# The turns of Q and K behind the last product with V and behind the ones pass, in a gated cross-attention and expert kernel

## The reference

```python
x = x + tanh(g_xattn) * attention(ctx, layernorm(x), b, seq_len)
x = x + tanh(g_ffn) * experts(layernorm(x), w1, b1, w2, b2, centroids, w_route)

logits = einsum('bhqd,bhkd->bhqk', Q * dh**-0.5, K) + b        # masked by seq_len
out = einsum('bhqk,bhkd->bhqd', softmax(logits), V)
```

## Time and profile before

| what | value |
|---|---|
| median of three runs | 1841.51 us |
| the profiled execution's own time | 1838.65 us |
| its span, first to last instruction | 1836.9 us |
| mean granted TensorE clock | 0.987 of full speed |
| TensorE busy with matmuls | 94% of the span |
| VectorE, ScalarE, GpSimd busy | 74%, 65%, 67% |
| from one ones pass to the next, steps with g = 0, 1, 2, 3 | 19.33, 19.12, 18.60, 18.57 us |

### The profile page before, as it was taken

The page is one execution under the profiler, slowest core; times in us unless marked ns, Lnnn a source line. Parts: engine busy times, 40 slices in busy tenths (PEclk is TensorE's granted clock), DMA queues, the critical chain, the costliest instruction groups (busy, mean ns, idle before and its releaser), DMA issues. The chain is left out here.

```text
span 1836.9 us, 33094 instructions
## 1 busy us (share of the span) xinstructions
PE 1718.4 (94%) x9714; PEld 1038.6 (57%) x9715; DVE 1364.6 (74%) x3007; ACT 1190.2 (65%) x2049; POOL 1224.8 (67%) x1395
## 2 busy tenths in 40 slices
PE   1699999999999999999999999999499999999997
PEld 1344545555555555555555555553378887878876
DVE  4677878878778788887887887773666776767765
ACT  4267677676776767767677676767256666666664
POOL 1257667585675857758577576654368888888886
PEclk9999999999999999999999999999599999999999
DMA  5979899898998989889889897974468888887784
GB/s 118 173 129 188 155 181 170 144 197 162 172 178 136 209 151 172 186 128 210 151 170 187 128 207 106 186 128 145 128 134 170 154 160 160 177 155 150 153 164 75
DMA packets 173099, 291.45 MB, mean 159 GB/s; under 512 B 38014, under 2 KB 42110, under 8 KB 172976
## 3 DMA queue, kind: packets, MB, share of 16 engines
q1 hardware_dynamic: 138704, 219.88, 62.1%
q0 software_dynamic: 32960, 67.68, 18.5%
q10 hardware_dynamic: 1312, 2.38, 0.8%
HBM read 127.09 MB, written 71.63 MB: 108 GB/s over the span
## 5 line engine op out<-in xcount | busy, mean ns | idle before, releaser
L1157 DVE TENSOR_REDUCE bank<-bank 128x1 f32<-128x512 f32 x1024 | 696.0, 690 | 255.0 <-PE bank L906 246.9
L751 ACT ACTIVATE prob<-bank 128x512 f32<-128x512 f32 x1024 | 593.1, 597 | 355.2 <-PE bank L894 354.1
L655 POOL TENSOR_TENSOR prob<-prob 128x512 f32<-128x512 f32 x252 | 315.8, 1294 | 319.0 <-PE bank L828 319.0
L894 PE MATMUL bank<-stB,stack_a_then_w_hi 100*128 100x512 f32 x1024 | 476.0, 466 | 16.0 <-ACT prob L751 13.7
L906 PE MATMUL bank<-stack_a_then_w_hi,stB 98*128 98x512 f32 x1024 | 423.1, 415 | 35.0 <-DMA stack_a_then_w_hi<-regrouped_then_w 19.7
L894 PEld LDWEIGHTS bank<-stB,stack_a_then_w_hi 100*128 100x128 f32 x1024 | 193.2, 189 | 248.4 <-ACT prob L751 176.3
L659 POOL TENSOR_TENSOR prob<-prob 128x512 f32<-128x512 f32 x252 | 315.5, 1295 | 0.0
L828 PE MATMUL bank<-prob,vin 128*32 128x512 f32 x2048 | 272.7, 605 | 0.7 <-ACT prob L751 0.7
L1429 POOL DMA_INDIRECT out_dram<-yout,scatter_ids x144 | 227.8, 1582 | 50.2 <-issue 38.1
L906 PEld LDWEIGHTS bank<-stack_a_then_w_hi,stB 98*128 98x128 f32 x1024 | 197.8, 193 | 84.7 <-DVE bank L1157 40.0
L1402 POOL DMA_INDIRECT rows_in<-xn_rows,gather_ids x152 | 181.6, 1195 | 71.5 <-issue 43.7
(11 more groups left out here) (202 smaller groups left out, 2160.7 us busy)
## 6 DMA issues: line engine op xcount, KB each, us to landing
stB<-regrouped_then_w SPq DMA_DIRECT2D x192, 256.0 KB, 5.7
stack_a_then_w_hi<-regrouped_then_w SPq DMA_DIRECT2D x183, 256.0 KB, 6.5
x_k_then_w<-in_x_dram SPq DMA_DIRECT2D x16, 1024.0 KB, 7.9
x_k_then_w<-in_ctx_dram SPq DMA_DIRECT2D x16, 1024.0 KB, 11.0
vin<-in_ctx_dram SPq DMA_DIRECT2D x16, 1024.0 KB, 8.7
xres<-in_x_dram SPq DMA_DIRECT2D x16, 1024.0 KB, 6.4
out_dram<-xres SPq DMA_DIRECT2D x16, 1024.0 KB, 7.2
xn_rows<-xn SPq DMA_DIRECT2D x60, 256.0 KB, 5.4
```

The lines of the kernel that those rows point to most:

```text
L655: pool.tensor_tensor(first[:, j, :], first[:, j, :], more[:, j, :], ALU.add).then_inc(s_acc, 1)
L751: act.activation(prob_of(st, 0, u)[:, j, :], psS[j % 2][:, :], ACT.Exp).then_inc(s_exp, 1)
L894: pe.matmul(psS[j % 2][:, :], stA[0:100, g, j, kt * P:(kt + 1) * P], stB[0:100, g, j, :], start=True, stop=True).then_inc(s_qk, 1)
L1157: dve.tensor_reduce(mx[:, s // 4, s % 4:s % 4 + 1], psM[s % 2][:, :], AX.X, ALU.max).then_inc(s_mx, 1)
```

## The change

The turn of Q moves from slot 0 to slot 1, where it stands behind the product with V. The turn of K moves from slot 3 to slot 2, where it stands behind the ones pass. ScalarE's copy of the turned Q moves from slot 0 to slot 1 and VectorE's low part of Q from slot 1 to slot 2; both keep their places for K. Nothing is added or taken away.

```diff
@@ ScalarE
-                        if s in (0, 4) and st.on(3):
+                        if s in (1, 4) and st.on(3):
                             evac_turned(st, s // 4)
@@ TensorE
                             values(st, -1, NT - 1)
                         if s == 2 and st.on(-1):
                             sums(st, -1)
-                        if s in (0, 3) and st.on(3):
-                            turn_rows(st, s // 3)
+                        if s in (1, 2) and st.on(3):
+                            turn_rows(st, s - 1)
@@ VectorE
-                        if s in (1, 5) and st.on(3):
+                        if s in (2, 5) and st.on(3):
                             lo_part(st, s // 5)
```

## The result

The changed kernel takes 1876.04 us (median of four runs, 1874.39 to 1876.36), the kernel before on the same occasion 1841.15 us: a ratio of 1.0189, 95% interval 1.0176 to 1.0203. That is 34.9 us slower. The profiled execution has a span of 1874.6 us.

What follows compares the result with a forecast made beforehand. TensorE was taken as the engine to follow, held in runs of three pairs by ScalarE and VectorE. Terms 16.1 (TQ) + 19.2 (TK) + 1 (fill) = 36.3 us gave 1877.8 us, range 1860 to 1889 (own range 1869 to 1886).

Steps and rivals of the forecast that it cites:

- The run of three costs what the turn saves: Step's border and behind the ones pass: third pair waits for its readers, so leaving out TQ saves 0.08 us, TK 0.07.
- The step 61 of the kernel before: Step with all pairs but no TQ or TK, taken as model: 1.93 us slot 15 to V, 3.82 ones pass to V.
- The turn behind narrow tiles adds 0.39 us: Behind V and the ones pass: V to turn 0.99, turn to next product 0.41, 1.40 us together against 1.00.
- The kinds of step: TQ at the border: +0.31 us in ordinary steps, +0.06 into g = 2, +0.39 into g = 1; TK +0.32 everywhere.
- The first steps: Steps 1 to 60 priced by g alone, fifteen of each kind for TQ, 0.32 us each for TK.
- The fill: Steps -3 to 0: TK waits for VectorE, 1 to 1.5 us per step; priced 0 to 5 us together, 1 taken.
- TK finds its bank free: Behind the ones pass: VectorE's low part of Q frees TQ's bank 0.4 us before TK's turn, so no wait.
- The base: Profiled execution's 1838.65 us plus 36.3 gives 1874.95; the median of runs lies 2.86 us higher, giving 1877.8.
- The rival with one costly place: Only one of the two places hurts, so only TK's 19 us remain: 1861 us, chance 0.12.
- the bank's wait: Rival: TK waits 0.3 us for TQ's bank in each of 60 steps, +18 us, 1896 us; chance 0.09.
- the rival of a full TensorE: Order is only bookkeeping; each of 120 turns saves 0.45 us and costs 0.39: -7 us, 1834.3 us, chance 0.04.

Runs made afterwards that it cites:

- q_only: Against the kernel before, only the turn of Q moves behind the V product, with its copy and low part; K keeps slot 3: 1858.19 us against 1841.56.
- k_only: Against the kernel before, only the turn of K moves behind the ones pass; Q keeps slot 0: 1858.08 us against 1841.56.
- q_ahead_of_v: Against the kernel before, Q is turned in slot 1 ahead of the V product, its copy and low part as in q_only; K keeps slot 3: 1868.85 us, ratio 1.0156.
- after_short_both: Changed kernel with maxima and exponentials over 128 of 512 columns only: 1809.92 us, against 1767.13 us for the kernel before with the same edits.

## Why the prediction was right, point by point

The forecast was 1877.8 us, the measured time 1876.04.

- *The run of three costs what the turn saves* (0.08 of 0.45 us left for Q, 0.07 for K). Right to 0.01 us in the rows of after (from slot 15 to V 1.93 us, from the ones pass to V 4.20 for 4.21), and shown as a cause: with both readers short and the transfers light, no wait is left and the sign turns over. The step 61 of the kernel before had been a fair model.
- *The turn behind narrow tiles adds 0.39 us.* Right: V to the turn 0.99, turn to the next product 0.41. In after the weight load of the turn behind V starts with the turn (702.27 and 702.28), while that of a turn between pairs starts 0.23 us ahead of it (682.09 and 682.32 in before). The rule of the Trainium skill (TensorE: Matmul & The Clock Gate, the table at its head) that weight loads are pulled ahead of the matmuls in flight, weighed against my price, would have made the sum 6 us smaller; it holds between pairs here and not behind V.
- *The kinds of step*. Into g = 2 it came at +0.39 for +0.38 in all, with the 0.33 us of saving at the border. Into g = 1 I had taken no saving, +0.71, and it was +0.65. Of these 0.06 us, q_only has 0.01 (its turn of Q adds 0.38) and k_only 0.03 (its turn of K adds 0.29 there), so my reading of the border, no saving, was right. Over the stage this makes 0.6 to 0.9 us too much.
- *The first steps.* Steps 1 to 4 lack the turns of XT and LG. I priced them like the others. Steps 2 and 3 came at +0.3 us instead of 0.63 (18.74 us for 18.43 in step 2), but steps 1 and 5 at +0.57 and +0.62 instead of 0.38. Together that is only 0.2 us too much: these errors cancel, which is luck.
- *The fill.* Its 1 us came near by luck. The first ones pass starts at 102.25 instead of 101.39 us, +0.86, where 1 for the fill and 0.39 for the border of step 1 had been priced. The wait of TK that I had in it was not there: in step -2 of the changed kernel TK starts at 41.50 while VectorE's low part of Q runs only from 42.35 to 43.03. Up to step 0 there is no ones pass to take a bank, so TQ and TK use different ones (`turn_table`, L132). Step 0 even starts 1.6 us earlier (79.29 for 80.88). It takes 0.95 us longer to slot 0 of step 1 (18.22 us for 17.27), and then the clock falls: from 98 to 101 us the granted clock is 0.50, behind 1.27 us of waiting for a transfer, and V takes 1.76 us until the turn of Q (99.44 to 101.20) instead of 0.99. Slot 0 of step 1 is 4.74 us ahead of its ones pass, in an ordinary step of the same kernel 3.43 us, so the fall cost about 1.3 us. q_only, with +2.1 us, has the same fall there; k_only, with -0.3, waited 1.91 us and has none.
- *TK finds its bank free.* Right: 0.4 us of slack forecast, 0.46 measured. The bank was no part of the cost.
- *The base.* By the profiled executions the changed part cost 33.9 us in the stage and 0.86 ahead of it, 34.8 together, so the sum of 36.3 was 1.5 us too large; the medians differ by 34.9. The profiled execution of before ran 2.5 us under its median. Added to it, the sum would have given 1874.95, 1.1 us too little; added to the median it gave 1.8 too much. Either base served.

The rival with one costly place fell with q_only and k_only; the bank's wait fell with the slack; the rival of a full TensorE holds only for readers faster than TensorE. What my picture lacked hardly counts in the change itself: the clock's fall, once at step 1 here and four times in another order, and how near the transfers into the stacks are to binding.

## What to carry to other kernels

Where an engine makes pieces for two readers through double banks, ask how many pieces in a row it makes without other work, and what a reader needs for one: here TensorE needs 0.46 us for a pair, the readers 0.60 to 0.65, so the third pair in a row waits, and other work between pairs is nearly free. Moving such work next to a piece it seems to fit saves its own 0.06 us and gives the filled wait back. A last step of a pipeline that lacks the moved operation is an experiment already made: read its distances, start to start, before building anything.

## What the runs showed that I had not expected

- A turn has three prices: 0.45 us between pairs, 0.39 behind V, 0.45 ahead of V. The V product on its 128x32 tiles starts 0.53 us behind a turn, a full-width product 0.36 us; behind V the turn itself comes after 0.99 us, as any product does, and only its successor is 0.05 us late. The change had picked the cheapest of the three places and lost all the same.
- In q_ahead_of_v the granted clock fell to its lower level in four steps of one kind, 1.6 us each, behind an idle stretch of 0.49 us that the steps without a fall have too. An order that looked 0.06 us per step dearer was 9.5 us dearer. In after_short_both it fell in eight steps.
- With short readers the transfers into the stacks come near to binding: the old order keeps steps of 17.7 us with 1.3 us of waits for them between 200 and 1100 us, while the changed order, with 15.0 us of such waits, has most of its steps at 17.6 to 18.5 us. The shortest full steps of the real kernels, 18.6 and 19.2 us, are by my estimate about 1 us away from that.
- One VectorE operation of 0.7 us, moved by one place into idle time, was worth 15 us, nearly half of what the studied change cost.
